# One scan and one weighting for both tiles of a step in a fused FFN, Mamba, FFN kernel

## The reference, cut to what matters

```python
x = x + 0.5 * ffn(layernorm(x))
x = x + mamba(layernorm(x))
x = x + 0.5 * ffn(layernorm(x))

def ffn(x):      # xr, xk: x mixed with the token before it
    return sigmoid(xr @ W_r.T) * (square(relu(xk @ W_k.T)) @ W_v.T)

def mamba(x):    # 1024 inner channels, 16 states for each
    xs, z = split(layernorm(x) @ W_in.T)
    xc = silu(b_conv + conv4(xs))
    dt_low, B, C = split(xc @ W_xproj.T)
    delta = softplus(dt_low @ W_dt.T + b_dt)
    for t in tokens:
        h = exp(delta[t] * A) * h + delta[t] * B[t] * xc[t]
        y[t] = sum_over_states(h * C[t])
    return ((y + D_skip * xc) * silu(z)) @ W_out.T + x
```

## Time and profile before

| | |
|---|---|
| median of 3 runs | 5426.3 us (5424.6 to 5429.3) |
| the profiled execution | 5428.4 us, its span 5426.3 us |
| DVE busy | 4967.8 us, 92% of the span |
| PE busy | 4474.0 us, 82% |
| ACT busy | 3031.2 us, 56% |
| POOL busy | 2906.2 us, 54% |
| granted TensorE clock, mean | 0.905 of full speed |
| DMA | 810.8 MB, 149 GB/s |

### The profile page before, as it was taken

The page is one execution under the profiler, slowest core; times in us unless marked ns, Lnnn a source line. Parts: engine busy times, 40 slices in busy tenths (PEclk is TensorE's granted clock), DMA queues, the critical chain, the costliest instruction groups (busy, mean ns, idle before and its releaser), DMA issues.

```text
span 5426.3 us, 59521 instructions
## 1 busy us (share of the span) xinstructions
PE 4474.0 (82%) x16640; PEld 2497.0 (46%) x16640; DVE 4967.8 (92%) x5826; ACT 3031.2 (56%) x6291; POOL 2906.2 (54%) x2111
## 2 busy tenths in 40 slices
PE   6677888888888878888888888878888788888788
PEld 2344544444454444545444444444544444444443
DVE  2899999999999999999999999999999999999993
ACT  2555655555555555555556555555655656555552
POOL 1545556465565545555455564555555455554661
PEclk9878999898999989999998989989999898998888
DMA  1545555454554545555455554556556565554651
GB/s 64 154 122 166 156 164 157 124 173 142 172 154 149 156 137 168 157 155 164 131 165 152 171 155 140 155 139 171 154 149 169 135 168 155 168 154 117 168 162 64
DMA packets 423066, 810.80 MB, mean 149 GB/s; under 512 B 41264, under 2 KB 41264, under 8 KB 418640
## 3 DMA queue, kind: packets, MB, share of 16 engines
q1 hardware_dynamic: 422736, 807.00, 52.0%
HBM read 772.25 MB, written 34.60 MB: 149 GB/s over the span
## 4 chain that ended last, share of the span: by engine, by line
DVE 49%; PE 22%; issue 16%; ACT 8%; DMA 2%; POOL 2%; DVEq 1%; SPq 0%; POOLq 0%; ACTq 0%
DVE decay L1065 22%; DVE g L1075 13%; PE mm L420 5%; DVE xc L1019 4%; PE y_acc L504 4%; PE mm L431 4%; PE mm L446 3%; PE mm L409 2%; PE mm L527 2%; DVE xc L1029 2%; PE mm L456 2%; DVE mix_k L996 2%; ACT rows L662 2%; DMA res_scratch<-rows 2%; DVE xn_col L1001 2%
## 5 line engine op out<-in xcount | busy, mean ns | idle before, releaser
L1284 POOL TENSOR_TENSOR dbx<-u,b_all 128x1024 f32<-128x1024 f32 x1024 | 2413.5, 2360 | 2131.8 <-DVE decay L1065 2130.6
L1065 DVE TENSOR_TENSOR_SCAN decay<-decay,state,dbx 128x512 f32<-128x512 f32 x2048 | 2619.8, 1279 | 172.6 <-ACT decay L849 171.0
L504 PE MATMUL y_acc<-ident,g 128*128 128x128 f32 x8192 | 1220.3, 291 | 372.5 <-DVE g L1075 359.6
L849 ACT ACTIVATE decay<-delta,neg_a 128x512 f32<-128x512 f32 x2048 | 1415.5, 692 | 68.4 <-ACT state L855 0.4
L504 PEld LDWEIGHTS y_acc<-ident,g 128*128 128x128 f32 x8192 | 1005.6, 149 | 922.9 <-DVE g L1075 578.8
L1075 DVE TENSOR_TENSOR g<-decay,c_all 128x512 f32<-128x512 f32 x2048 | 1374.9, 671 | 7.6 <-PE y_acc L504 7.6
L855 ACT ACTIVATE state<-decay 128x1 f32<-128x1 f32 x2048 | 340.6, 167 | 1519.3 <-DVE g L1075 1517.5
L431 PE MATMUL mm<-wbuf_c,col 128*128 128x512 f32 x1024 | 459.9, 593 | 0.9 <-DVE rows L1008 0.9
L409 PE MATMUL mm<-mix_k,wbuf_c 128*128 128x512 f32 x512 | 293.4, 728 | 118.2 <-ACT col L727 76.8
L446 PE MATMUL mm<-xn_col,wbuf_a 128*128 128x512 f32 x512 | 302.1, 746 | 68.4 <-ACT delta L808 48.5
L446 PE MATMUL mm<-xn_col,wbuf_d 128*128 128x512 f32 x512 | 290.4, 720 | 72.2 <-ACT col L727 70.5
(11 more groups left out here) (92 smaller groups left out, 4557.8 us busy)
## 6 DMA issues: line engine op xcount, KB each, us to landing
b_all<-bc_scratch SPq DMA_DIRECT2D x1024, 256.0 KB, 3.8
c_all<-bc_scratch SPq DMA_DIRECT2D x1024, 256.0 KB, 4.5
wbuf_c<-in_w_v SPq DMA_DIRECT2D x32, 1024.0 KB, 7.8
wbuf_d<-in_w_r SPq DMA_DIRECT2D x16, 1024.0 KB, 6.7
xin<-in_x SPq DMA_DIRECT2D x16, 1024.0 KB, 10.3
wbuf_c<-in_w_k SPq DMA_DIRECT2D x16, 1024.0 KB, 8.2
wbuf_d<-in_w_in SPq DMA_DIRECT2D x16, 1024.0 KB, 7.5
wbuf_a<-in_w_in SPq DMA_DIRECT2D x16, 1024.0 KB, 10.4
```

Of the source, the lines that this page charges most:

```text
L504: last = pe.matmul(y_acc[:, tb, j * P:(j + 1) * P], g[:, m % GRING, tb * P:(tb + 1) * P], ident[:, :], start=n == 0 and j == 0 and tb % 2 ...
L849: act.activation(decay[:, m % DBANKS, :], delta[:, q % 2, j, :], ACT.Exp, scale=neg_a[:, QT * q + j, n:n + 1]).then_inc(decay_done, 1)
L1065: dve.tensor_tensor_scan(d, d, dbx[:, s % DBX, j, :], state[:, batch, m:m + 1], ALU.mult, ALU.add).then_inc(scan_done, 1)
L1284: pool.tensor_tensor(dbx[:, s % DBX, :, :], u[:, q % 2, :, :], b_all[:, s % BRING, :].unsqueeze(1).broadcast_to([P, QT, W]), ALU.mult).the ...
```

## The change

A step is now one unit in place of two.
- `scan` runs once over 1024 columns. The decay at the first column of the second tile is set to 0, and the true carry (decay times old state) is added to `dbx` at that column. So the second tile starts afresh inside the same scan.
- ACT's `make_decay` issues three instructions for a step: exp of 512 columns, a copy of one zero, exp of 511 columns. `save` copies both tiles' last columns at once. New `lead_decay` makes the 16 first-column decays of a quarter.
- POOL's `product` is followed by a small instruction that adds the carry to one column of `dbx`, and `make_u` by one that multiplies the 16 carries with the old states. `product` now waits for `mult_done` of the step four before, in place of `scan_done`.
- DVE's step is now `scan(s)`, the other work, `weigh(s)`.
- `decay` has two pairs of banks (four banks), `mm` two banks in place of three. `g` has two pairs in place of four singles. `GROUPS` and all the lists have new steps and banks.
- `ffn_relu2` waits for the mix of its own tile. `head` comes ahead of the three taps.

```diff
-        decay = ps("decay", [P, DBANKS, W])
-        mm = ps("mm", [P, 3, W])
+        decay = ps("decay", [P, PAIRS, QT, W])
+        mm = ps("mm", [P, 2, W])
...
-            def sum_g(it, m):
+            def sum_g(it, s):
...
-                for tb in range(TB):
-                    last = pe.matmul(y_acc[:, tb, j * P:(j + 1) * P], g[:, m % GRING, tb * P:(tb + 1) * P],
+                for j in range(QT):
+                    for tb in range(TB):
+                        last = pe.matmul(y_acc[:, tb, j * P:(j + 1) * P], g[:, s % PAIRS, j, tb * P:(tb + 1) * P],
...
-                act.wait_ge(f_dve[i].sem, f_dve[i].at(k, "xr3"))
+                act.wait_ge(f_dve[i].sem, f_dve[i].at(k, f"xr{j}"))
...
+            def lead_decay(k, q):
+
+                if due(count := 2 * (NSTEP * k + NS * (q - 1))):
+                    act.wait_ge(dbx_done, count)
+                act.wait_ge(h_act.sem, h_act.at(k, f"xb{q}"))
+                act.activation(carry[:, q % 2, :], neg_a[:, QT * q + 1, :], ACT.Exp,
+                               scale=delta[:, q % 2, 1, 0:1]).then_inc(h_act.sem, 1)
...
+                if due(count := NSTEP * it + s - PAIRS + 1):
                     act.wait_ge(saved, count)
-                act.activation(decay[:, m % DBANKS, :], delta[:, q % 2, j, :], ACT.Exp,
-                               scale=neg_a[:, QT * q + j, n:n + 1]).then_inc(decay_done, 1)
+                d = decay[:, s % PAIRS, :, :]
+                e = QT * q
+                act.activation(d[:, 0, :], delta[:, q % 2, 0, :], ACT.Exp,
+                               scale=neg_a[:, e, n:n + 1]).then_inc(decay_done, 1)
+                act.activation(d[:, 1, 0:1], zero[:, :], ACT.Copy).then_inc(decay_done, 1)
+                act.activation(d[:, 1, 1:W], delta[:, q % 2, 1, 1:W], ACT.Exp,
+                               scale=neg_a[:, e + 1, n:n + 1]).then_inc(decay_done, 1)
...
-                dve.wait_ge(decay_done, NM * it + m + 1)
-                d = decay[:, m % DBANKS, :]
-                dve.tensor_tensor_scan(d, d, dbx[:, s % DBX, j, :], state[:, batch, m:m + 1],
+                dve.wait_ge(decay_done, 3 * (NSTEP * it + s + 1))
+                d = flat(decay[:, s % PAIRS, :, :])
+                dve.tensor_tensor_scan(d, d, flat(dbx[:, s % DBX, :, :]), state[:, batch, s, 0:1],
                                        ALU.mult, ALU.add).then_inc(scan_done, 1)
...
-                dve.tensor_tensor(g[:, m % GRING, :], decay[:, m % DBANKS, :], c_all[:, s % CRING, :],
+                dve.tensor_tensor(g[:, s % PAIRS, :, :], decay[:, s % PAIRS, :, :],
+                                  c_all[:, s % CRING, :].unsqueeze(1).broadcast_to([P, QT, W]),
                                   ALU.mult).then_inc(mult_done, 1)
...
                     if scn:
-                        scan(it, 2 * s, bt)
-                    if s > 0:
-                        if scn:
-                            weigh(it, 2 * s - 1)
-                    elif back:
-                        weigh(b, NM - 1)
-                    if scn:
-                        scan(it, 2 * s + 1, bt)
-                        weigh(it, 2 * s)
+                        scan(it, s, bt)
...
+                    if scn:
+                        weigh(it, s)
...
-            def make_u(k, q):
+            def make_u(k, q, batch):
...
+                pool.wait_ge(h_act.sem, h_act.at(k, f"lead{q}"))
+                pool.tensor_tensor(carry[:, q % 2, :], carry[:, q % 2, :], state[:, batch, NS * q:NS * q + NS, 1],
+                                   ALU.mult).then_inc(h_pool.sem, 1)
...
-                if due(count := NM * it + QT * (s - DBX + 1)):
-                    pool.wait_ge(scan_done, count)
+                if due(count := NSTEP * it + s - DBX + 1):
+                    pool.wait_ge(mult_done, count)
...
+                pool.wait_ge(dbx_done, 2 * (NSTEP * it + s) + 1)
+                pool.tensor_tensor(dbx[:, s % DBX, 1, 0:1], dbx[:, s % DBX, 1, 0:1], carry[:, q % 2, n:n + 1],
+                                   ALU.add).then_inc(dbx_done, 1)
```

More of the change, by code:

```diff
@@ L221, in bank_free @@
                     return None
-        def earlier(m):
-            if m >= DBANKS:
-                return m - DBANKS, 0
-            return max(p for p in range(NM) if p % DBANKS == m % DBANKS), 1
         def flat(t):
@@ L350, in body @@
                         sp.dma_start(wbuf["b"][:, :, :], piece(w_in, 0, E + 512)).then_inc(wz_loaded[1], 16)
-                    if front and s == 51:
+                    if front and s == 50:
                         after(mark(m_act, f, "xp"))
@@ L360, in body @@
                         sp.dma_start(wbuf["a"][:, :, :], piece(w_out, 0, 0)).then_inc(wo_loaded[0], 16)
-                    if ahead and s == 55:
+                    if ahead and s == 54:
                         if front:
@@ L603, in body @@
+                    if scn and s == 31:
                         z(it, 2, slot)
-                    if scn and s == 35:
-                        sum_skip(it, 2)
+                    if back and s == 33:
+                        for ct in range(CT):
+                            ffn_turn(it, 1, b, ct)
+                    if scn and s == 34:
                         dt_proj(it, it, 3, 0)
                         dt_proj(it, it, 3, 1)
-                    if scn and s == 37:
+                        sum_skip(it, 2)
@@ L648, in _ @@
             act.wait_ge(init_dve, 2)
[L649 removed]
+            act.wait_ge(init_pool, 12)
             def ffn_norm(i, k, fronted=True):
@@ L893, in body @@
-                    if scn and s == 5:
+                        if s == 3:
+                            ffn_before_k(0, f, 0)
+                            ffn_before_k(0, f, 1)
+                    if scn and s == 4:
                         softplus(it, 1, 0)
                         softplus(it, 1, 1)
-                    if front and s in (5, 6):
-                        ffn_before_r(0, f, 2 * (s - 5), xn_col[:, other, :, :])
-                        ffn_before_r(0, f, 2 * (s - 5) + 1, xn_col[:, other, :, :])
@@ L899, in body @@
-                    if front and 9 <= s < 13:
-                        ffn_relu2(0, f, s - 9)
-                    if scn and s == 11:
+                        lead_decay(it, 1)
+                    if front and s == 5:
+                        ffn_before_k(0, f, 2)
+                        ffn_before_k(0, f, 3)
+                        ffn_before_r(0, f, 0, xn_col[:, other, :, :])
+                    if front and s == 6:
+                        for ct in (1, 2, 3):
+                            ffn_before_r(0, f, ct, xn_col[:, other, :, :])
@@ L902, in body @@
+                    if front and 7 <= s < 11:
+                        ffn_relu2(0, f, s - 7)
+                    if front and 11 <= s < 15:
+                        ffn_tanh(0, f, s - 11)
+                    if scn and s == 12:
                         skip_columns(it, 1)
-                    if front and 13 <= s < 17:
-                        ffn_tanh(0, f, s - 13)
+                    if scn and s == 15:
+                        softplus(it, 2, 0)
+                        softplus(it, 2, 1)
+                        lead_decay(it, 2)
@@ L905, in body @@
                     if scn and s == 17:
                         keep_y(it, 0)
-                    if scn and s == 19:
-                        softplus(it, 2, 0)
-                        softplus(it, 2, 1)
-                    if front and s == 26:
+                    if front and s == 25:
                         mamba_inner(f)
@@ L934, in body @@
                     if back and s == 34:
-                        ffn_columns(1, b, 3, front)
+                        for ct in range(CT):
+                            ffn_columns(1, b, ct, front)
                         ffn_lead(1, b, bb)
-                    if scn and s == 34:
-                        gate_tanh(it, 2)
-                    if back and s in (35, 36):
-                        ffn_before_k(1, b, 2 * (s - 35), front)
-                        ffn_before_k(1, b, 2 * (s - 35) + 1, front)
@@ L963, in body @@
+                    if front and s == 51:
                         softplus(f, 0, 0)
                         softplus(f, 0, 1)
-                    if back and s in (53, 54):
+                        lead_decay(f, 0)
+                    if back and 52 <= s < 55:
                         ffn_tanh(1, b, s - 51)
@@ L1306, in body @@
                     if scn and s == 43:
-                        make_u(it, 3)
+                        make_u(it, 3, bt)
+                    if front and s == 58:
+                        make_u(f, 0, (bt + 1) % BATCHES)
                     if back and 59 <= s < 63:
                         ffn_add(1, b, s - 59)
-                    if front and s == 60:
-                        make_u(f, 0)
                     if ahead and s == 63:
```

445 lines of the change are left out of this document (193 added, 252 removed).

## The result

The changed kernel takes 5152.7 us in the median (5150.9 to 5167.4) against 5425.6 us before in the same comparison. The ratio is 0.950, with a 95% interval of 0.948 to 0.952. I had said 5022 us, with a range of 4890 to 5210. The direction was right and the time lies in the range, but a third of the forecast gain is missing: 273 us came, 404 were forecast.

The account below looks back on a forecast made before the run. DVE was taken to bound the kernel (92% busy), with PE near (82%). DVE's list shrinks by 8.6 + 19.4 - 1 = 27 us, an iteration by 26.5; 15 x 26.5 + 8 = 405 us gives 5022 us, range 4890 to 5210.

Parts of the forecast that it names:

- Part 2: POOL's product begins behind the weighting, so DVE instructions with two SBUF operands are hardly held: 19.4 us less an iteration.
- Part 1: DVE's fused scan and weighting: scan 2.39 us, weighting 1.17 us, together 8.6 us less an iteration.
- empty step: A DVE step with no other work than scans and weighting: 3.56 us before, 3.50 us forecast.
- Part 4: Shorter ring of decays: ACT's slack 1.6 us against about 0.85, DVE's idle time stays at 16 us, plus 1.
- Part 5: Two mm banks for PE's groups: with a reader one step behind, this costs nothing where ACT and DVE are on time.
- rival (d): Two banks bind: PE's groups of steps 4 to 26 wait 1.6 us each, iteration 339 us, 5610 us; chance 0.05.
- rival (a): PE sets nearly everything, steps 48 to 62 too: iteration about 312 us, 5190 us; chance 0.15.
- The rule of the Trainium skill: The next DVE operation waits until the pipe is empty; without its exception, fusing alone would bring 22 us an iteration.

Follow-up runs that it names:

- e1: The changed kernel with one wait put back, so that POOL's product waits for scan_done in place of mult_done: 5449.6 us, ratio 1.004.
- e2: The kernel before with one wait changed, so that POOL's product waits for one scan more (no fusing, three mm banks, old lists): 5156.0 us, ratio 0.950.
- e6: The changed kernel, where ffn_r and ffn_v of the chunk ahead leave out the fourth quarter of the contraction: 5080.2 us, ratio 0.935.
- e4: The changed kernel with an exponential in place of softplus for delta, so that ACT needs one function table: 5117.4 us, ratio 0.943.
- e8: The kernel of e3 with keep_y ahead of x_rows at step 49, and f1T and f1k alternating between both mm banks in the last three iterations: 5079.6 us.
- e3: The changed kernel, where the eight xs groups ahead of the first chunk's scans alternate between both mm banks: 5110.6 us, ratio 0.942.

## Why the prediction was right, and where its size was off

**Part 2 was right, and it is nearly the whole gain.** It was put at 19.4 us an iteration. Taking it away costs 19.1 us (324.27 - 305.13, e1). Adding it alone to the kernel before brings 18.0 (327.44 - 309.46, e2), the price of one edited wait. DVE's own work changes by 17.1 us in the first pair and 21.7 in the second. Both gains come where the forecast placed them, in steps 4 to 8 and 27 to 47.

**Part 1 was right in its durations and wrong in what they bring.** The fused instructions take 2.35 + 1.22 us and an empty step 3.53 (3.50 forecast). DVE's work falls by 12.1 us an iteration with fusing and new lists (e1's 299.16 against 311.24). Some 3.1 of them are not fusing: by the rows of lines, the held instructions of e1 (`conv_silu`, both mixes, `head`) cost 591 us in the run against 641 before. That leaves 9.0, where 8.6 were forecast. But the iteration falls by 3.2 only. The rest came back as idle time: e1's DVE idles 25.1 us in an iteration where before it was 16.2. By stretch, from e2 to the changed kernel 1.7 us are won in steps 0 to 3, 0.5 in 4 to 8 and 5.8 in 9 to 26, and 1.1 and 2.6 us are lost in 27 to 47 and 48 to 63.

**Part 4 is the step that failed in the iteration.** It said that ACT's slack doubles, so that DVE's idle time stays at 16 us, plus 1. It rose by 7, to 23.1, and the waits for decays rose by as much (171 to 289 us in the run). DVE's work came out 2 us below the forecast, so this term is all that the iteration lacks. I had counted ACT's own work behind the weighting of s-2, but not that ACT's list stands still for PE with the next `save` and decays behind it. Such a wait in the changed kernel, step 49 on ACT and what follows on DVE:

```profile
1957.19 0.68 ACT L754 ACTIVATE xdbl<-mm,xscale 64x512 f32<-64x512 f32 x1 [3.51 <-PE mm L455]
1957.77 1.06 ACT L802 ACTIVATE y_rows<-y_acc 128x512 f32<-128x512 f32 x2
1958.73 0.16 ACT L829 ACTIVATE state<-decay 128x2 f32<-128x2 f32 x1
1958.92 0.69 ACT L820 ACTIVATE decay<-delta,neg_a 128x512 f32<-128x512 f32 x1
```

```profile
1960.41 2.36 DVE L1030 TENSOR_TENSOR_SCAN decay<-decay,state,dbx 128x1024 f32<-128x1024 f32 x1 [1.32 <-ACT decay L823]
```

The weighting that `save` needed had ended at 1955.57 (1954.34 + 1.23 in the timeline). ACT's waits for PE grew: `ffn_tanh`, 173 us before, is 247 us now, and `gate_tanh` 279 (55 before). Two runs say more. These are the waits of DVE on decays and of `ffn_tanh` on PE, in e1 and then in e6:

```profile
DVE decay L1030 <- ACT decay L823: 289.9, 147, 9.5
ACT rows L696 <- PE mm L407: 246.5, 114, 4.7
```

```profile
DVE decay L1030 <- ACT decay L823: 217.8, 136, 9.5
ACT rows L696 <- PE mm L407: 190.2, 100, 5.5
```

In e1 an iteration takes 324.3 us and the waits are as long as in the changed kernel. So they do not come from DVE being faster; they came with the rewritten step, its lists and its rings, and no run separates these. In e6 PE has 16 matmul records fewer and ACT's list is untouched, and the waits for decays fall by 71 us, 4.4 an iteration. So ACT's standing still for PE is at least that part of them. e4 took away as much by removing the table loads.

The prediction's own stretches compare as follows: 102 us for steps 4 to 26 (100.8 measured), 115 for 27 to 47 (118.2), 84 for 48 to 3 (86.2). The first one, where PE's pace was reckoned, is right to 1%, and e6 shows that PE holds it up. The other two lack 5 us of waiting.

**Part 5 is the step that failed outside the iteration, and it is half of what is missing.** It said that two banks cost nothing, since a reader stands one step behind its group. That holds where scans and the the other bank's groups lie between the groups of one bank. It does not in the lead-in, where no scans run, and in the last piece, where the front work is absent: there each group waits for its bank. Of the 10.5 us that e8 gave back, 3.3 came while the last chunk's scans ran and 7.3 behind them. I had read the iteration and multiplied it by 15, and never followed the new bank numbers through the iterations at the ends. `GROUPS` has all eight xs groups in bank 0. This was rival (d)'s mechanism at another place: the lead-in is 41.6 us longer (e3 gives it all back), and the last piece 10 us longer where 8 less were forecast (e8 gives all of it back).

The account of spans: 14 middle iterations at 22.3 us are 312 us, chunk 0 gave 17.8, and 41.6 + 10 went at the ends. That is 278 us, the difference of the spans. Against the forecast, some 60 us are missing in the middle, 9 in chunk 0, 42 in the lead-in and 18 at the end.

The measured 5153 us lie nearer to rival (a)'s 5190 than to the forecast's 5022, but not by (a)'s mechanism: its iteration was 312 us and the measured one is 305, and the rest was lost at the ends, which neither counted. In rival (d), 15 iterations of 339 us would give 5600 us, not 5610.

The rule of the Trainium skill ("VectorE: DVE Perf Modes", section on the DRAIN), taken without its exception, would have made fusing worth 22 us an iteration. The scan and weighting before already overlapped, and fusing brought 3.2 us together with all the new lists.

## What to carry to other kernels

Before fusing instructions to save their fixed part, look for instructions whose mean is far above their shortest, and see which other engine runs beside the long ones: here moving one wait by one scan was worth as much as rewriting five engines' lists. When a change takes buffers from a side path, follow the buffer's sequence through the first and last iterations as well, where the work that hid the waits is absent. And when the busiest engine gets 9% less work, price the wait of every in-order list behind the second busiest, not only that engine's own time.

## What the runs showed of the hardware that was not expected

A three-column addition with two SBUF operands is held by POOL's product as a long one is. The line of `head` in e1, with its shortest, median and longest duration in ns:

```profile
L982 DVE TENSOR_TENSOR xc<-xc,head x128: 142/153/1898, 104.1 to 4981.9; 128x3 f32<-128x3 f32 x128
```

It works the other way too: in the changed kernel POOL's one-column add took 0.52 us in the median of the 198 that ran beside a DVE instruction with two SBUF operands, and 0.19 us in the median of the others. The same eight matmul records took 3.67 us or 6.6 us in the lead-in, according to whether 0.27 or 3.6 us of waiting lay between the groups: a wait of PE also made the work behind it dearer.
